# A projection of rounded products, and a quantised feed-forward with its steps spread over POOL and ACT

## The reference, cut to what matters

```python
def bitlinear(x, W, b):
    w_scale = jnp.clip(jnp.mean(jnp.abs(W)), EPS, None)
    Wq = _ste(W, jnp.clip(jnp.round(W / w_scale), -1.0, 1.0) * w_scale)
    x_scale = jnp.clip(jnp.max(jnp.abs(x), axis=-1, keepdims=True), EPS, None)
    xq = _ste(x, jnp.clip(jnp.round(x * (QB / x_scale)), -QB - 1.0, QB) * (x_scale / QB))
    return jnp.einsum('bnd,hd->bnh', xq, Wq) + b
h = bitlinear(x, W1, b1)                      # x: layer norm of the tokens, h: 1024 wide
h = jax.nn.gelu(h, approximate=False)
x = x + bitlinear(h, W2, b2)
...
ln = layernorm(layernorm(x), ln_l_g, ln_l_b)
q = ln @ Wq.T                                 # third block: q, k, v of the tokens, 768 columns
kv = jnp.concatenate([xn @ Wkv.T, ln @ Wlkv.T], axis=1)
```

## Time and profile before

| what | value |
| --- | --- |
| median of three runs | 926.93 us |
| profiled execution, its own time | 928.22 us |
| its span | 926.5 us |
| PE, DVE, ACT, POOL busy in the span | 94%, 68%, 57%, 42% |
| feed-forward and projection in the span | about 53 to 194 us |

### The profile page before, as it was taken

How to read it: one execution, slowest core, us unless ns; L and a number is a source line. 1 busy time by engine, 2 the same in 40 slices (tenths; PEclk the granted TensorE clock), 3 DMA queues, 4 the chain that set the end, 5 groups by cost and what they waited for, 6 DMA issues and landing times.

```text
span 926.5 us, 14997 instructions
## 1 busy us (share of the span) xinstructions
PE 866.8 (94%) x4299; PEld 611.3 (66%) x4300; DVE 630.7 (68%) x1275; ACT 532.6 (57%) x851; POOL 388.9 (42%) x334
## 2 busy tenths in 40 slices
PE   9977789889999999999999999999999999999992
PEld 4635455545555555555457887878888888888881
DVE  5788987855567557456488779846666666666666
ACT  2558885445665765775554534326666666666650
POOL 2144455435676746756515545512222222222210
PEclk9999999989999999999999999999999999999997
DMA  9400000009478578569565100078711298526405
GB/s 310 110 1 1 0 1 1 1 5 364 160 292 328 194 305 326 219 269 350 199 262 196 82 1 1 12 316 342 305 40 36 71 348 341 208 88 254 116 9 182
DMA packets 49909, 154.07 MB, mean 166 GB/s; under 512 B 6266, under 2 KB 24438, under 8 KB 44236
## 3 DMA queue, kind: packets, MB, share of 16 engines
q1 hardware_dynamic: 46124, 144.25, 41.4%
q0 software_dynamic: 3744, 9.31, 3.1%
HBM read 97.85 MB, written 56.62 MB: 167 GB/s over the span
## 4 chain that ended last, share of the span: by engine, by line
PE 67%; DVE 17%; ACT 6%; issue 3%; DMA 3%; POOL 2%; SPq 1%; DVEq 0%; ACTq 0%; POOLq 0%
PE banks L1047 11%; PE banks L1300 8%; PE banks L1302 8%; PE banks L1301 8%; PE banks L1015 4%; PE banks L1039 3%; PE banks L1040 3%; DVE small L2105 2%; PE banks L1337 2%; PE banks L1339 2%; PE banks L1338 2%; PE banks L1313 2%; PE banks L953 2%; PE banks L919 1%; PE banks L1061 1%
## 5 line engine op out<-in xcount | busy, mean ns | idle before, releaser
L1047 PE MATMUL banks<-wexp 128*65 128x512 f32 (+1 forms) x288 | 149.9, 602 | 3.5 <-ACT wexp L1614 3.5
L677 POOL TENSOR_TENSOR cv_hl<-wexp,cv_hl 128x1024 fp32r<-128x1024 f32 x45 | 108.6, 2421 | 56.0 <-ACT cv_hl L1591 55.4
L1300 PE MATMUL banks<-ring,x_hi 128*128 x312 | 127.5, 408 | 0.0
L1302 PE MATMUL banks<-ring,x_lo 128*128 x312 | 122.1, 391 | 0.0
L1301 PE MATMUL banks<-ring,x_hi 128*128 x312 | 122.0, 391 | 0.0
L1614 ACT ACTIVATE wexp<-banks 128x512 f32<-128x512 f32 x128 | 76.4, 599 | 64.2 <-PE banks L1040 63.8
L2105 DVE TENSOR_REDUCE small<-banks 128x1 bf16<-128x1107 f32 x64 | 84.1, 1314 | 38.4 <-PE banks L1015 38.4
L1750 ACT ACTIVATE banks<-wexp 128x1024 f32 x72 | 73.5, 1021 | 47.7 <-DVE aux L2496 47.7
L1728 ACT ACTIVATE aux<-banks 128x512 f32<-128x512 f32 x78 | 46.7, 599 | 61.2 <-PE banks L1302 45.2
L1039 PE MATMUL banks<-q_hi,k_hl 128*128 128x512 f32 x144 | 76.7, 533 | 1.9 <-ACT q_lo L1582 1.0
L1302 PEld LDWEIGHTS banks<-ring,x_lo 128*128 128x128 f32 x312 | 58.6, 188 | 13.2
(11 more groups left out here) (374 smaller groups left out, 2171.5 us busy)
## 6 DMA issues: line engine op xcount, KB each, us to landing
wsplit<-cv_hl SPq DMA_DIRECT2D x45, 1024.0 KB, 8.0
ring<-wsplit SPq DMA_DIRECT2D x32, 1280.0 KB
wexp<-in_L_ffn_w SPq DMA_DIRECT2D x40, 512.0 KB, 5.9
wexp<-in_expert_biases SPq DMA_DIRECT2D x8, 1152.0 KB, 6.6
ring<-wsplit SPq DMA_DIRECT2D x4, 1024.0 KB, 8.2
wexp<-moe_y SPq DMA_DIRECT2D x7, 512.0 KB, 6.1
wexp<-in_L_ffn_sw SPq DMA_DIRECT2D x5, 512.0 KB, 9.0
x_sb<-in_x SPq DMA_DIRECT2D x4, 512.0 KB, 7.6
```

What stands on the lines that cost most here:

```text
L677: g.tensor_tensor(sides(hl[:, PIECE:2 * PIECE]), raw, sides(hl[:, 0:PIECE]).bitcast(f32), ALU.subtract).then_inc(s['cv_lo'], 1)
L1047: mm(pb[5 + half][0:DA, :], vh[b][0:w, c, :], pT[q % 3][0:w, :], start=c == 0, stop=c == len(KTILES) - 1).then_inc(s['a_pv'], 1)
L1300: mm(o[:], x_hi[u][:, kc, :], hi, start=kc == 0 and not primed, stop=False, skip_group_check=primed)
L1302: last = mm(o[:], x_lo[u][:, kc, :], hi, start=False, stop=primed and kc == KC - 1, skip_group_check=primed)
```

## The change

The rounded copies of tokens and weights, `l_hi` and `w_hi` (type float32r, written by ACT), and what is left, `l_lo` (DVE) and `w_lo` (POOL), make the projection three products instead of one float32 product. Tiles are turned and copied out in pairs. In the feed-forward, POOL rounds the tokens (`ffn_tokens`), and adds the block's result (`ffn_result`), which ACT has copied out of bank 6 with its scale (`ffn_sum` is now ACT's); the transposes of the tokens stand between `ffn_out` and `ffn_hidden_T` of the turn before. DVE's statistics go to the end of a turn and to tile i-2. The projections in `between` stand one turn later. `ln_r` of tiles 8 to 15 comes from ACT's root and `norm`. The constants of the third block go into POOL's loop. Left out below: semaphore names, counts of `const`, shapes.

```diff
@@ -135,6 +135,9 @@
...
+        _, l_hi, l_lo, w_hi, w_lo = aliased(("x_span16", XS), *((n, KC * 4 * P) for n in ("l_hi", "l_lo")), *((n, KC * QKV) for n in ("w_hi", "w_lo")))
...
@@ -190,6 +193,7 @@
+        y_part = [scr.take(D) for _ in range(2)]
...
@@ -386,6 +391,11 @@
+        W_LOW_AT = (7, 9)
+        def pair_at(p):
+            return slice(p % 2 * 2 * P, (p % 2 + 1) * 2 * P)
...
@@ -608,16 +618,42 @@
+            def ffn_tokens(t):
+                g.tensor_scalar(xn[:, t % 2, :], xn[:, t % 2, :], f_by[:, t % 2, 0:1], MAGIC, ALU.mult, ALU.add).then_inc(s['f_xm'], 1)
+            def ffn_result(t):
+                pool.wait_ge(s['f_yout'], t + 1)
+                g.tensor_tensor(x_sb[:, t, :], x_sb[:, t, :], y_part[t % 2], ALU.add).then_inc(s['f_res'], 1)
+            def attention_constants(k):
+                if k == 4:
+                    link(g.memset(o_hi[DH:P, :].bitcast(f32), 0.0))
+                elif k % 2:
+                    link(g.memset(k_hi[k // 2][DH:DA, 0:S + SK].bitcast(f32), 1.0))
+                else:
+                    link(g.memset(k_hl[k // 2][:, S + SK:KW].bitcast(f32), 0.0))
+                    link(g.memset(vh[k // 2][:, :, DH:DA], 1.0))
...
-                g.tensor_scalar(xn[:, t % 2, :], x_sb[:, t, :], mv[:, t, 0:1], rstd[:, t:t + 1], ALU.subtract, ALU.mult).then_inc(s['f_xn'], 1)
+                g.tensor_scalar(xn[:, t % 2, :], x_sb[:, t, :], rstd[:, t:t + 1], less_mean[:, t:t + 1], ALU.mult, ALU.add).then_inc(s['f_xn'], 1)
+                if t >= 1:
+                    pool.wait_ge(s['f_by'], t)
+                    ffn_tokens(t - 1)
+                if t in W_LOW_AT:
+                    pool.wait_ge(s['w_pre'], 3)
+                    kc = W_LOW_AT.index(t)
+                    g.tensor_tensor(w_lo[:, kc, :], wT[:, kc, :], w_hi[:, kc, :].bitcast(f32), ALU.subtract).then_inc(s['w_pre'], 1)
...
-                if t >= 5:
-                    pool.wait_ge(s['f_by'], t)
...
+                if t >= 6:
+                    ffn_result(t - 6)
+                if 8 <= t < 13:
+                    pool.wait_ge(s['f_res'], t - 5)
+                    attention_constants(t - 8)
...
@@ -629,13 +665,10 @@
-            for u in range(2):
-                link(g.memset(k_hl[u][:, S + SK:KW].bitcast(f32), 0.0))
-                link(g.memset(k_hi[u][DH:DA, 0:S + SK].bitcast(f32), 1.0))
-                link(g.memset(vh[u][:, :, DH:DA], 1.0))
-            link(g.memset(o_hi[DH:P, :].bitcast(f32), 0.0))
+            for t in range(T - 6, T):
+                ffn_result(t)
...
@@ -895,13 +928,15 @@
-            pe.wait_ge(s['f_pre'], 2)
-            def ffn_in(t, u):
+            pe.wait_ge(s['w_pre'], 2)
+            def ffn_tokens_T(t, u):
...
+            def ffn_in(t, u):
...
@@ -932,46 +967,56 @@
+                if there(i + 4):
+                    ffn_tokens_T(i + 4, u)
...
-            def proj_in(t):
-                pe.wait_ge(s['l_xh'], t + 1)
-                if t > 0:
-                    pe.wait_ge(s['l_xT'], t)
+            def proj_in(p):
+                pe.wait_ge(s['l_xh'], 2 * p + 2)
+                if p > 0:
+                    pe.wait_ge(s['l_xT'], 2 * p)
...
-                    last = tr(pb[7][:, kc * P:(kc + 1) * P], xn[:, t % 4, kc * P:(kc + 1) * P], ident[:])
+                    for u in range(2):
+                        at = (kc * 2 + u) * P
+                        last = tr(pb[7][:, at:at + P], xn[:, (2 * p + u) % 4, kc * P:(kc + 1) * P], ident[:])
...
             def proj_part(t, k):
+                p = t // 2
...
-                    pe.wait_ge(s['l_xT'], t + 1)
+                    if t == 0:
+                        pe.wait_ge(s['w_pre'], 2 + 1 + KC)
+                    pe.wait_ge(s['l_xT'], 2 * p + 1)
...
+                o, at = pb[PROJ_BANK[t % 2] + k][:, 0:n], slice(t % 4 * P, (t % 4 + 1) * P)
...
-                    last = mm(pb[PROJ_BANK[t % 2] + k][:, 0:n], xnT[:, kc, t % 4 * P:(t % 4 + 1) * P], wT[:, kc, a:a + n], start=kc == 0, stop=kc == KC - 1)
+                    mm(o, l_hi[:, kc, at], w_hi[:, kc, a:a + n], start=kc == 0, stop=False)
+                    mm(o, l_hi[:, kc, at], w_lo[:, kc, a:a + n], start=False, stop=False)
+                if k == 0:
+                    pe.wait_ge(s['l_xlo'], p + 1)
+                for kc in range(KC):
+                    last = mm(o, l_lo[:, kc, at], w_hi[:, kc, a:a + n], start=False, stop=kc == KC - 1)
...
-                if t + 2 < T:
-                    proj_in(t + 2)
+                if t % 2 == 0 and t + 2 < T:
+                    proj_in(t // 2 + 1)
...
             def between(i):
                 if i == -3:
-                    warm(WARM_FFN)
+                    warm(WARM_FFN, pb[5])
                 if i == T - 4:
...
-                    proj_in(1)
-                    pe.wait_ge(s['f_acc'], T - 1)
-                    proj(0)
                 if i == T - 3:
...
-                if T - 3 <= i < T:
-                    proj(i - T + 4)
+                if T - 3 <= i <= T:
+                    proj(i - T + 3)
...
@@ -1468,12 +1513,12 @@
             def times(k, raw):
...
-                a(flat(q), flat(raw), ACT.Sign, bias=cols[:, 32:33]).then_inc(s['f_pre'], 1)
+                a(flat(q), flat(raw), ACT.Sign, bias=cols[:, 32:33]).then_inc(s['w_pre'], 1)
...
@@ -1516,51 +1561,63 @@
-                if there(tokens):
+                if isinstance(tokens, int) and tokens == T - 1:
...
+            def ffn_sum(t, u):
+                act.wait_ge(s['f_y'], t + 1)
+                act.wait_ge(s['f_by'], t + 5)
+                if not isinstance(t, int) or t >= 2:
+                    act.wait_ge(s['f_res'], t - 1)
+                a(y_part[u], pb[6][:, 0:D], ACT.Copy, scale=f_step[:, 1 - u, 1:2]).then_inc(s['f_yout'], 1)
             def ffn_turn(i, u):
-                if there(i + 3):
-                    ffn_T(i + 3, 1 - u)
+                if there(i - 1):
+                    ffn_sum(i - 1, 1 - u)
...
-            def proj_T(t):
-                act.wait_ge(s['l_xT_full'], t + 1)
-                if t >= 4:
-                    act.wait_ge(s['l_qkv'], t - 3)
-                for kc in range(KC):
-                    last = a(xnT[:, kc, t % 4 * P:(t % 4 + 1) * P], pb[7][:, kc * P:(kc + 1) * P], ACT.Identity,
-                             scale=lg[:, kc:kc + 1], bias=lb[:, kc:kc + 1])
-                last.then_inc(s['l_xT'], 1)
+                if there(i + 4):
+                    ffn_T(i + 4, u)
+            def proj_T(p):
+                act.wait_ge(s['l_xT_full'], p + 1)
+                if p >= 2:
+                    act.wait_ge(s['l_qkv'], 2 * p - 2)
+                for to in (l_hi, xnT):
+                    for kc in range(KC):
+                        last = a(to[:, kc, pair_at(p)], pb[7][:, kc * 2 * P:(kc + 1) * 2 * P], ACT.Identity,
+                                 scale=lg[:, kc:kc + 1], bias=lb[:, kc:kc + 1])
+                    last.then_inc(s['l_xT'], 1)
...
-                if t + 2 < T:
-                    proj_T(t + 2)
+                if t % 2 == 0 and t + 2 < T:
+                    proj_T(t // 2 + 1)
...
                 if i == -4:
...
+                    act.wait_ge(s['ld_l1'], NLD['ld_l1'])
+                    a(flat(w_hi), flat(wT), ACT.Copy).then_inc(s['w_pre'], 1)
                 if i == -3:
...
                 if i == T - 4:
...
-                    proj_T(1)
-                if T - 3 <= i < T:
-                    proj_kept(i - T + 3)
+                if T - 2 <= i <= T:
+                    proj_kept(i - T + 2)
...
+            root(LN_EARLY, T)
...
@@ -1796,7 +1853,7 @@
-            def norm(c0, c1, guard):
+            def norm(c0, c1, guard, to=rstd):
...
@@ -1806,9 +1863,9 @@
-                link(v.reciprocal(d, t_))
...
+                link(v.reciprocal(to[:, c0:c1], t_))
...
@@ -1909,7 +1966,7 @@
             def ffn_scales(t0, t1):
...
-                ve.sem_inc(s['f_rstd'], 1)
+                v.scalar_tensor_tensor(less_mean[:, t0:t1], mv[:, t0:t1, 0], -1.0, rstd[:, t0:t1], ALU.mult, ALU.mult).then_inc(s['f_rstd'], 1)
...
@@ -1982,29 +2039,24 @@
-            def ffn_sum(t, u):
-                ve.wait_ge(s['f_y'], t + 1)
-                ve.wait_ge(s['f_pool'], t + 1)
-                v.scalar_tensor_tensor(tile(t), pb[6][:, 0:D], f_step[:, 1 - u, 1:2], tile(t), ALU.mult, ALU.add)\
-                    .then_inc(s['f_yout'], 1)
             def ffn_statistics(t):
-                ve.wait_ge(s['f_yout'], t + 1)
-                statistics(t)
+                ve.wait_ge(s['f_res'], t + 1)
+                return statistics(t)
...
             def ffn_turn(i, u):
-                if there(i - 1):
-                    ffn_sum(i - 1, 1 - u)
...
+                    if not isinstance(i, int) or i >= 2:
+                        ve.wait_ge(s['f_yout'], i - 1)
...
-                    if not there(i + 1):
+                    if isinstance(i, int) and i < 0:
...
-                if there(i - 1):
-                    ffn_statistics(i - 1)
```

(52 more changed lines are left out.)

33 lines of the change are left out of this document (18 added, 15 removed).

## The result

The changed kernel takes 932.45 us (median of 20 runs, 929.58 to 935.02), the one before 928.31 (20 runs, 925.69 to 931.85): a ratio of 1.004, 95% interval 1.0031 to 1.005. The forecast was 931.2 against 926.93, +4.3; measured is +4.1. The sum is right, but its two large terms are not: the feed-forward gained 2.5 us where +2.3 was forecast, and the projection and the maxima lost 4.4 where +2.0 was.

The account below looks back on a forecast made before the run. The prediction took the feed-forward as bound by DVE and ACT, the projection by PE and DVE. Feed-forward -1.9 + 3.7 + 0.5 = +2.3 and projection +2.0 made +4.3 us: 931.2 us against 926.93, range 921 to 938.

Parts of the forecast that it names:

- Plain turns: Feed-forward turns where POOL has no extra work: 4.1 us each, 4.33 before; together 1.9 us less.
- POOL's bursts: Feed-forward rounds of tiles 7 to 12: low-weight subtractions and constants make POOL late and hold back turns, +3.7 us.
- the shared port: POOL and DVE shutting each other out in the feed-forward: nothing in the sum, 2.4 us at the upper end.
- The forecast's own sign: POOL's token rounding expected near 0.84 us; at 0.75 or below the feed-forward forecast is too high.
- The start: Start of the feed-forward pipeline: ACT's root for tiles 8 to 15 waits behind tile 1's turned tokens, +0.5 us.
- The projection: Projection through the eight maxima: saved matmul time outweighed by later starts and waits, +2.0 us; bounds -2.8 and +5.0.
- the start of projection 3: In the tail, PE starts this tile's projection 18.8 us after hidden row 14; before, 16.64.
- the 2.4 us of waits of PE between projections 3 and 8: In the projection, PE waits 2.4 us for the low parts and for the tokens of tile 9.
- The clock falls: Rival: PE's clock drops to its lower level in feed-forward turns with long fills; +16, 943 us; chance 0.09.
- Its row: Evidence for a falling clock: PE busy 1.69 of 4 us from 62 to 66, granted clock 0.57 from 70 to 74.
- The products pay: Rival: POOL keeps pace in the feed-forward, low parts are ready in the projection; -4.2, 922.7 us; chance 0.19.
- Its feed-forward half: Part of a rival: POOL's multiply-and-add costs near 0.73 us and the fills fit its idle time, -1.4 us.

Follow-up runs that it names:

- third run: Changed feed-forward with the float projection of the kernel before, no low halves or low weights: 924.91 us, 0.9976 of the kernel before.
- second run: Changed kernel with POOL's norm of a row put back to subtract and multiply: 933.01 us, 1.0057 of the kernel before.
- The seventh: Changed kernel with the five groups of constant memsets moved behind POOL's rounds: 933.77 us, 1.0064 of the kernel before.
- ninth run: Changed kernel with the 12 warming matmuls put ahead of the transposes of tile 1's tokens: 933.3 us, 1.005 of the kernel before.
- fifth run: Changed kernel with DVE's context squares moved from behind tile 4 to behind tile 5: 930.14 us, 1.0023 of the kernel before.
- the tenth: Changed kernel with 11 and 7 matmuls of ones filling two PE waits in the tail: 929.43 us, 1.0015 of the kernel before.
- sixth run: Changed kernel without the product of the tokens' high part and the weights' low part: 931.59 us, 1.004 of the kernel before.
- first run: Changed kernel with one more register instruction per expert step, a clamp shared by all the experiments: 931.33 us, 1.0048 of the kernel before.

## Why the prediction held, and where it did not

**Plain turns** (forecast 4.1 each, -1.9): too high. In the changed kernels a turn without extras takes 3.94 to 4.18, and one more gain was not foreseen: before's turn from 72.30 to 77.64 took 5.34 because of the clock of 0.57 in the earlier trace rows; the same turn is 3.95 after. It alone is 1.4 of the 2.5 us gained. Without `w_lo` (third run) row 1 to 14 is 4.0 us below before's, so the turns gave twice what the forecast took for them.

**POOL's bursts** (+3.7): the step that failed. It took the extra work of POOL (7.6 us in six rounds) as time of the turns, from a POOL already nearly full. The rounding was half the price and the norm less than half; but by the second run even 8.6 us more of POOL cost only 0.4. What the bursts do cost comes by another way, the shared port, which the forecast had at nothing:

```profile
88.67 1.29 DVE L2040 SCALAR_TENSOR_TENSOR wexp<-banks,small,wexp 128x1024 f32<-128x1024 f32 x1
...
89.18 1.83 POOL L649 TENSOR_TENSOR w_lo<-wexp,w_hi 128x768 fp32r<-128x768 f32 x1
...
90.20 0.83 DVE L2054 TENSOR_TENSOR small<-small 128x2 f32<-128x2 f32 x1
...
92.44 1.01 POOL L632 MEMSET k_hi<- 1x1101 f32 x1
92.52 0.95 DVE L2033 TENSOR_SCALAR small<-small 128x2 f32<-128x2 f32 x1
...
93.68 1.28 DVE L2040 SCALAR_TENSOR_TENSOR wexp<-banks,small,wexp 128x1024 f32<-128x1024 f32 x1
```

Two steps of DVE on two columns, 0.15 to 0.17 us when free, end with POOL's `w_lo` and with its memset, and this turn lasts 5.01. By the third run the low weights cost 1.5 us. The seventh, without the memsets, gains 0.65, but this is no second cost: with the memsets and without `w_lo` the turns are 4.0 to 4.1. So the bursts cost about 1.5 us together, not 3.7. The forecast's own sign, a rounding at 0.75 us or below, had said that its feed-forward would be too high. The Trainium skill (SBUF — State Buffer, Who interferes with whom) says that a DVE instruction with two SBUF inputs contends with GpSimd's reads, and one in a two-port mode with GpSimd altogether, the later one blocked until the first has ended; the rows of L2054 and `w_lo` agree with the first half; those of L2033 agree with the second if it runs in such a mode, which no row shows, whereas L1976 at 90.06 of the earlier trace rows, the same step, did not wait.

**The start** (+0.5): against before's 68.1, row 1 stands at 67.9 to 68.7 in four of nine profiled executions with this start and at 69.7 to 69.9 in five, so the term is about 0 or +1.7. The forecast counted ACT's root and did not see that PE's warming matmuls had come behind a wait of 3.3 us for POOL. As the ninth run did not turn this into time, how much of the median it makes is open.

**The projection** (+2.0): direction right, size not. The products (L996 at 147.04 to L996 at 149.22, a tile in 2.18 us) and the start of projection 3 (140.69, 18.2 behind row 14, forecast 18.8) were right. The term that failed is the 2.4 us of waits of PE between projections 3 and 8: they are 1.43 + 0.58 + 2.17 = 4.2. The 2.17 is the context's squares, longer by POOL's squares on the same port (the product took 1.12 and 0.50 us, the tokens behind them 1.08 for 0.40); and the clock that fell cost some 1.4 more (154.53 to 158.66 is 4.1 us for transposes and a tile that take 2.7 at the full clock). The fifth run takes away the wait, the tenth the low clock behind it; neither profile has its maxima earlier for it, counted from row 14.

**The rivals.** "The clock falls" was right in that waits bring the low level, though not every time, and wrong in its place: not in the steady turns, where POOL was to be the bound, but behind single waits of 1.2 to 3.3 us at the start, in the tail and in attention's first step, where it costs 1 to 3 us each. Its row was of this kind: from 62 to 66 us, with PE busy 1.69 of 4, the clock was 1.00; the 0.57 came behind a later wait of PE.

```profile
69.83 1.61 PE L919 MATMUL banks<-ident,wexp 128*128 128x128 f32 x8 [2.75 <-ACT wexp L1522]
```

"The products pay" does not fit the sixth run: without a third of them nothing was gained, and PE only waited longer. Its feed-forward half had the right direction and half the size (-1.4 for -2.5).

**Why the sum held.** -2.5 in the feed-forward, +4.2 to the maxima, +0.2 in them and +0.2 in attention's first step is +2.1 by the profiles (and -0.8 in the rest of the span, where nothing was changed). The other 2 us of the medians stand in no single profile. The candidates are the start (up to 1.8), the rest of the span (720.7 to 723.3, and 721.2 in the profile of the changed kernel) and the stretch from row 14 to the maxima, which is 54.8 us in the changed kernel and in the first run, and 55.6 and 57.3 in two others in which nothing of it was changed. The forecast did not have these terms; its errors were +4.8 in the feed-forward and -2.4 behind it, and with this gap of 2 they left 0.2. So the total came out by luck: two wrong terms of opposite sign, and a difference between executions that the forecast did not have.

## What to carry to other kernels

Before an engine's extra work is charged to a pipeline, look for the idle time that it spends waiting for the stage it feeds: with 16 us of it, POOL took on 8.6 us more for 0.4 of the stage. When a wide, slow matmul is replaced by several short ones, PE's time saved becomes waits, and the waits cost a second time through the clock; see first that the copies and subtractions that feed them come early. And two gains and losses that cancel look like no change: separate the halves by building the kernel with only one of them, which here was 0.2 to 0.3% faster than the kernel before, and 0.5% with its waits filled.
